# ScalarE copies the recurrence's norms out of PSUM and its kk rows into PSUM, in place of VectorE

## What is computed

```python
sa = jnp.einsum('bhij,bhj->bhi', state, -kk_t)
state = w_t[..., None] * state + sa[..., None] * (kk_t * a_t)[:, :, None, :] + k_t[..., None] * v_t[:, :, None, :]
norm = jnp.sqrt(jnp.mean(state * state, axis=-1, keepdims=True))
state = state / (norm + EPS_STATE)
o_t = jnp.sum(state * r_t[..., None], axis=-1)
```

## Time and profile before

| what | value |
|---|---|
| median of 3 runs | 2438.33 us (2436.32 to 2439.18) |
| the profiled execution's own time | 2441.28 us |
| its span in the profile | 2439.2 us |
| granted clock of TensorE, mean | 0.815 |
| VectorE busy | 2187.4 us (90% of the span) |
| ScalarE, GpSimd busy | 1585.6 us (65%), 903.2 us (37%) |

### The profile page before, as it was taken

The page is one execution under the profiler, slowest core; times in us unless marked ns, Lnnn a source line. Parts: engine busy times, 40 slices in busy tenths (PEclk is TensorE's granted clock), DMA queues, the critical chain, the costliest instruction groups (busy, mean ns, idle before and its releaser), DMA issues.

```text
span 2439.2 us, 47897 instructions
## 1 busy us (share of the span) xinstructions
PE 1925.3 (79%) x12321; PEld 1556.6 (64%) x12321; DVE 2187.4 (90%) x8800; ACT 1585.6 (65%) x5168; POOL 903.2 (37%) x1528
## 2 busy tenths in 40 slices
PE   5888888788888878888888878688887877344787
PEld 3555555455687867777777767677777767343555
DVE  6888887689619999999999999999999999999887
ACT  4878888577646665666666666666666565444776
POOL 0000000011105555555555555555555555555110
PEclk8999999699977787787877777987778777655899
DMA  5000000000000000000000000000000000000011
GB/s 183 17 17 22 17 21 23 3 1 1 1 1 1 1 1 1 1 1 1 1 1 1 1 1 1 1 1 1 1 1 1 1 1 1 1 1 1 1 35 35
DMA packets 14353, 25.02 MB, mean 10 GB/s; under 512 B 1280, under 2 KB 12032, under 8 KB 13824
## 3 DMA queue, kind: packets, MB, share of 16 engines
q1 hardware_dynamic: 14080, 21.97, 3.0%
HBM read 12.27 MB, written 4.19 MB: 7 GB/s over the span
## 4 chain that ended last, share of the span: by engine, by line
DVE 57%; issue 16%; PE 15%; ACT 6%; POOL 0%; DVEq 0%; POOLq 0%; ACTq 0%
DVE pn L1563 11%; DVE bank L1579 10%; DVE U L1620 8%; DVE xs L1551 5%; DVE bank L1568 5%; DVE kv L1612 4%; PE bank L282 3%; PE bank L267 2%; ACT prob L923 2%; PE bank L585 2%; DVE bank L1609 1%; PE bank L761 1%; DVE bank L1588 1%; DVE bank L1532 1%; PE bank L632 1%
## 5 line engine op out<-in xcount | busy, mean ns | idle before, releaser
L1748 POOL TENSOR_TENSOR wu<-U,stg 128x256 f32<-128x256 f32 x512 | 318.6, 622 | 682.2 <-DVE U L1620 682.2
L750 PE MATMUL bank<-U,ident 128*128 128x128 f32 x2048 | 464.2, 399 | 81.6 <-ACT go L1064 69.3
L750 PEld LDWEIGHTS bank<-U,ident 128*128 128x128 f32 x2048 | 426.7, 238 | 121.5 <-issue 90.6
L761 PE MATMUL bank<-stack,tm 128*128 128x64 f32 x1792 | 336.4, 374 | 145.7 <-ACT tm L994 137.2
L1213 ACT ACTIVATE xs<-U 128x128 f32<-128x128 f32 x1024 | 261.5, 302 | 275.5 <-DVE U L1620 271.6
L761 PEld LDWEIGHTS bank<-stack,tm 128*128 128x128 f32 x1792 | 325.6, 284 | 162.9 <-ACT tm L994 153.0
L1563 DVE TENSOR_REDUCE pn<-xs 128x16 f32<-128x256 f32 x1024 | 377.6, 408 | 0.6 <-issue 0.2
L1701 POOL TENSOR_TENSOR kv<-stg 128x256 f32<-128x256 f32 x513 | 318.7, 621 | 0.0
L1131 ACT ACTIVATE small<-pn 128x16 f32<-128x16 f32 x513 | 110.9, 216 | 295.0 <-DVE pn L1563 295.0
L735 PE MATMUL bank<-wcat,yT 128*128 128x224 f32 x1024 | 294.6, 447 | 2.5 <-issue 2.0
L1579 DVE TENSOR_TENSOR bank<-wu,bank 128x128 f32<-128x128 f32 x1024 | 292.0, 285 | 1.1 <-POOL wu L1748 0.8
(11 more groups left out here) (214 smaller groups left out, 3567.6 us busy)
## 6 DMA issues: line engine op xcount, KB each, us to landing
out_x<-x SPq DMA_DIRECT2D x8, 512.0 KB, 2.9
x<-in_x SPq DMA_DIRECT2D x1, 3584.0 KB, 17.7
Vs<-V SPq DMA_DIRECT2D x8, 384.0 KB, 4.6
Vs<-V SPq DMA_DIRECT2D x8, 288.0 KB, 3.3
lane<-in_lanes SPq DMA_DIRECT2D x8, 256.0 KB, 3.2
wcat<-in_wcat SPq DMA_DIRECT2D x1, 1792.0 KB, 13.2
wraw<-in_w_up SPq DMA_DIRECT2D x1, 1024.0 KB, 19.6
wraw<-in_w_down SPq DMA_DIRECT2D x1, 1024.0 KB, 11.4
```

The source lines that it names most:

```text
L750: last = pe.matmul(rsum.rearrange("p (t i) -> p t i", i=HD), ident[:, :], steps[:, :, :, j], start=(j == 0), stop=(j == HD - 1))
L761: last = pe.matmul(bank[3 + g][:, e * CH:(e + 1) * CH], tm[:, g * (PB // 2) + e, :, :].rearrange("p a c -> p (a c)"), stack[:, :], start=T ...
L1748: pool.tensor_tensor(ij(wu[:, :]), ij(U[:, half if j else 1 - half, (j - 1) % STEPS, :]), col(stg[:, half, j, TW, :]), ALU.mult).then_inc( ...
```

## The change

The `sring` ring is no longer copied. ScalarE takes the logarithm of its four rows where they lie, in PSUM, twice an iteration (`log_norms`). `stg` loses its kk part: ScalarE writes four kk rows from `R` straight to PSUM (`copy_kk`) and four rows of kk times a from `stg` to PSUM (`copy_kka`), each twice an iteration. All six stand behind the squares; each waits until VectorE has made both halves of `xs` of its step, and VectorE's first `zz` (L1568) of the same step waits for it, so that the two engines do not touch the bank at the same time. To make room, other work of ScalarE and GpSimd is moved: `retention(0)` from behind the squares of step 3 to those of step 0, `retention(1)` from behind those of step 5 to the front of those of step 1, `factors` from behind step 2's to the front of step 3's, the second part of `output_rms` to the front of step 5's, `evacuate_outputs` from the end of step 7 to behind the root of the next step 0; on GpSimd `retention_add` from step 4 to step 0.

```diff
@@ -181,10 +181,10 @@
         small = sb("small", [P, 3, HD], F32, late)
         lnr, rt, lam = (small[:, i, :] for i in range(3))
         zz = bank[0][:, 0:HD * HD]
-        kkz = bank[0][:, 256:384].rearrange("p (t q j) -> p t q j", q=2, j=HD)
-        sring = bank[0][:, 384:448].rearrange("p (t i) -> p t i", i=HD)
+        kkr = bank[0][:, 256:320].rearrange("p (t j) -> p t j", j=HD)
+        kkar = bank[0][:, 320:448].rearrange("p (g t j) -> p g t j", g=2, j=HD)
+        sring = bank[0][:, 448:512].rearrange("p (t i) -> p t i", i=HD)
         rsum = bank[7][:, 256:384]
-        hist = sb("hist", [P, 2, STEPS, HD], F32, late)
         rs = sb("rs", [P, STEPS, HD], F32, late)
         ge = sb("ge", [P, STEPS, 2 * HD], F32, late)
         gl = sb("gl", [P, STEPS, 2 * HD], F32, late)
...
@@ -1080,10 +1080,14 @@
                     act.wait_ge(O["ln"], i + 1)
                     act.activation(oss[:, 1, 0:1], oss[:, 1, 0:1], ACT.Exp, scale=0.5).then_inc(O["sd"], 1)
 
-            def stage_kk(half, row):
-
-                act.activation(stg[:, half, :, TKK, :], R[:, bass.ds(row, STEPS), QKK * HD:(QKK + 1) * HD],
-                               ACT.Copy).then_inc(G["kk"], 1)
+            def copy_kk(row):
+
+                act.activation(kkr, R[:, bass.ds(row, RENORM), QKK * HD:(QKK + 1) * HD], ACT.Copy).then_inc(S["kk"], 1)
+
+            def copy_kka(half, g):
+
+                act.activation(kkar[:, g, :, :], stg[:, half, g * RENORM:(g + 1) * RENORM, TKKA, :],
+                               ACT.Copy).then_inc(S["ka"], 1)
 
             def stage_kv(half, row):
                 act.activation(stg[:, half, :, TK:TV + 1, :].rearrange("p t q i -> p t (q i)"),
...
@@ -1108,11 +1112,14 @@
                     act.wait_ge(G["f1"], k)
                     act.activation(gl[:, :, :], ge[:, :, :], ACT.Ln, bias=1.0).then_inc(G["g2"], 1)
 
-            def log_norms(k, half, last):
-
-                act.wait_ge(S["h"], last)
-                act.wait_ge(G["f2"], k)
-                act.activation(ls[:, :, :], hist[:, half, :, :], ACT.Ln).then_inc(G["ls"], 1)
+            def log_norms(g):
+
+                act.activation(ls[:, g * RENORM:(g + 1) * RENORM, :], sring, ACT.Ln).then_inc(G["ls"], 1)
+
+            def beside_sums(t1):
+
+                for e in range(2):
+                    act.wait_ge(T[e]["x"], t1)
 
             def factors(k, half):
                 act.wait_ge(G["f2"], k + 1)
...
@@ -1186,53 +1193,70 @@
                         row_it = n % 2 * CH + m * STEPS
                         row_next = (n % 2 * CH + m * STEPS + STEPS) % (2 * CH)
                         for j in range(STEPS):
-                            root(t0 + (j + 1))
+                            t1 = t0 + (j + 1)
+                            jj, g = j % RENORM, j // RENORM
+                            root(t1)
                             if j == 0:
+                                if m >= 1:
+                                    evacuate_outputs(n, m - 1)
+                                elif n >= 1:
+                                    evacuate_outputs(n - 1, NB - 1)
                                 normalise(n, m)
+                                if m == 0 and ot is not None:
+                                    act.wait_ge(O["t1c"], (2 * ot + 2) * NB)
                                 stage_batch(n, m)
                             if j == 1:
-                                act.wait_ge(G["wc"], it + 1)
                                 gates(0, it, row_it)
                                 stage_kv(1 - half, row_next)
+                                retention(1, it + 1, row_next)
                             if j == 2:
                                 evacuate_projection(n, m, 0)
                             if j == 3:
+                                factors(it, 1 - half)
                                 evacuate_features(n, m)
                             if j == 4:
                                 row_sums(it)
                                 evacuate_projection(n, m, 1)
                             if j == 5:
                                 output_rms(n, m, 0)
+                                output_rms(n, m, 1)
                             if j == 6:
                                 stage_outputs(n, m)
                                 evacuate_pairs(n, m, 0)
                             if j == 7:
                                 evacuate_pairs(n, m, 1)
                             for e in range(2):
-                                act.wait_ge(T[e]["u"], t0 + (j + 1))
+                                act.wait_ge(T[e]["u"], t1)
                                 act.activation(xs[:, e, 1, :], rows8(U[:, half, j, :], e), ACT.Square).then_inc(T[e]["sq"], 1)
                             if j == 0:
                                 if n + 1 < NCH:
                                     act.wait_ge(C["rc"], (n + 1) * NB * 2 - 2 + 2 * m)
                                 else:
                                     act.wait_ge(C["rc"], NCH * NB * 2)
-                                stage_kk(1 - half, row_next)
-                            if j == 1:
-                                log_norms(it, 1 - half, it * 2 + 1)
-                            if j == 2:
-                                factors(it, 1 - half)
-                            if j == 3:
+                                act.wait_ge(G["wc"], it + 1)
                                 retention(0, it + 1, row_next)
                             if j == 4:
                                 gates(1, it, row_it)
-                            if j == 5:
-                                retention(1, it + 1, row_next)
-                                output_rms(n, m, 1)
-                            if j == 7:
-                                evacuate_outputs(n, m)
+                            if t1 < L and (j + 1) % RENORM == 1:
+                                beside_sums(t1 + 1)
+                                act.wait_ge(S["sg"], t1)
+                                act.wait_ge(G["f2"], it + (j + 1) // RENORM)
+                                log_norms(0 if j + 1 > RENORM else 1)
+                            if t1 < L and (j + 1) % RENORM == 2:
+                                beside_sums(t1 + 1)
+                                if t1 > RENORM:
+                                    for e in range(2):
+                                        act.wait_ge(T[e]["z"], t1 - 2)
+                                act.wait_ge(G["ka"], it + 1 + g)
+                                copy_kka(half if g == 0 else 1 - half, 1 - g)
+                            if t1 < L and (j + 1) % RENORM == 3:
+                                beside_sums(t1 + 1)
+                                copy_kk(row_it + RENORM if g == 0 else row_next)
             root(L + 1)
-            log_norms(L // STEPS, 1, L // RENORM + 1)
+            act.wait_ge(S["sg"], L + 1)
+            log_norms(1)
             factors(L // STEPS, 1)
+            evacuate_outputs(NCH - 1, NB - 1)
             act.wait_ge(O["ov"], L // STEPS + 1)
             for part in range(2):
                 i8 = slice(part * HD // 2, (part + 1) * HD // 2)
...
@@ -1546,27 +1562,27 @@
                             t1 = t0 + (j + 1)
                             if jj == 0:
                                 dve.wait_ge(S["kk"], it * 2 + (g + 1))
+                                dve.wait_ge(S["ka"], it * 2 + (g + 1))
                             for e in range(2):
                                 dve.wait_ge(T[e]["u"], t0 + j)
                                 dve.tensor_tensor(ij(xs[:, e, 0, :]), ij(rows8(U[:, half if j else 1 - half, (j - 1) % STEPS, :], e)),
-                                                  row(kkz[:, jj, 0, :], i=HD // 2), ALU.mult).then_inc(T[e]["x"], 1)
-                            if jj == 1:
-
-                                dve.wait_ge(S["sg"], t0 + j)
-                                if g == 0:
-                                    dve.tensor_copy(hist[:, 1 - half, RENORM:, :], sring).then_inc(S["h"], 1)
-                                else:
-                                    dve.tensor_copy(hist[:, half, 0:RENORM, :], sring).then_inc(S["h"], 1)
+                                                  row(kkr[:, jj, :], i=HD // 2), ALU.mult).then_inc(T[e]["x"], 1)
                             for e in range(2):
                                 dve.wait_ge(T[e]["x"], t1)
                                 dve.wait_ge(T[e]["sq"], t0 + j)
                                 dve.tensor_reduce(pn[:, e, :, :].rearrange("p a i -> p (a i)"),
                                                   xs[:, e, :, :].rearrange("p a (i j) -> p (a i) j", j=HD), AXX,
                                                   ALU.add).then_inc(T[e]["pn"], 1)
+                            if jj == 1:
+                                dve.wait_ge(G["ls"], it * 2 + (g + 1))
+                            if jj == 2:
+                                dve.wait_ge(S["ka"], it * 2 + (g + 2))
```

(20 more changed lines are left out.)

29 lines of the change are left out of this document (10 added, 19 removed).

## The result

The changed kernel takes 2445.22 us (median of 20 runs, 2437.44 to 2449.1) and the kernel before 2437.56 (20 runs, 2433.23 to 2441.24). The ratio is 1.0033, with the interval [1.0025, 1.0041]: slower by a third of a per cent. That is inside the range of the prediction, but 2 us above the 2443.2 up to which it called it the same.

The account below looks back on a forecast made before the run. Bound: a serial chain of steps, nearly all on VectorE, priced by how far instructions push off the next. Terms +12.2 - 10.5 - 2.6 + 1.3 + 0.3 = +0.7 us on the median of 2438.33 gave 2439.0 us, range 2432 to 2446.

Parts of the forecast that it names:

- the ends: Before the first step and at the end of the recurrence: +0.5 for a small operation, -0.2 for a norm copy gone.
- step 1: GpSimd's addition waits for ScalarE's exponential and delays `wu`: 3.13 us instead of 2.94, +12.2 us, bounds +9.6 and +16.0.
- steps 3 and 7: Row copies gone between reciprocal and product: 104 places at 0.06, 24 at 0.18, -10.5 us, bounds 0 and -18.7.
- step 5: Norm copy gone, but late squares hold the sums: 0.04 us won per iteration, -2.6 us, bounds 0 and -9.0.
- third wait of xs: Third semaphore at `xs` of steps 0 and 4: 0.01 us at 128 places, +1.3 us, bounds 0 and +3.8.
- Rival A: Product in steps 3 and 7 gains nothing, starting some 0.10 behind the reciprocal's end: 2445.2 us, chance 0.14.
- small delays that add up: Other delays, such as ScalarE late at step 0's squares or GpSimd slower to wake: 2443 to 2447 us, chance 0.08.
- rival D: Squares on time in step 5, so the whole 0.14 us is won there: 2432.6 us, chance 0.09.
- The steps costed at nothing: ScalarE's six new operations, hidden beside the sums before `zz`, and the moved `evacuate_outputs`, +1.6 us at most in 16 iterations.
- the prediction's own sign of error: If `zz` waits for ScalarE in steps 1 to 3 or 5 to 7, something taken as hidden is not.
- B: The addition doesn't hold `wu`, step 1 is 2.80 us and +12.2 becomes -9.0: 2417.8 us, chance 0.03.
- C: Each VectorE copy taken away in steps 3, 5 and 7 gives back all its drawn time: 2404.1 us, chance 0.02.

Follow-up runs that it names:

- few_waits: Changed kernel without the two kk row waits at the first `xs` of steps 0 and 4, except the very first: 2441.2 us, ratio 1.0008 to the kernel before.
- add_late: Changed kernel with GpSimd's `retention_add` moved from behind step 0's outer product to behind step 1's: 2424.12 us, ratio 0.9942 to the kernel before.
- wait_alone: Kernel before, all VectorE copies kept, with only both retention operations and GpSimd's `retention_add` moved as in the change: 2449.98 us, ratio 1.0050.
- u_first: Changed kernel with all three waits of `xs` in steps 0 and 4 kept, the state's written first: 2438.86 us, ratio 1.0004 to the kernel before.
- best: both_evac with the root's two waits turned round and, at the sums, the wait for the squares written before that for `xs`: 2388.61 us, ratio 0.9811.
- norms_only: Kernel before with only the norm copies removed, ScalarE taking the logarithm straight from `sring`; no retention moved: 2423.2 us, ratio 0.9939.
- root_order: Kernel before with ScalarE's root waiting for the sums of half 1 first in the code, then half 0: 2413.02 us, ratio 0.9912.
- both_evac: Changed kernel with `retention_add` behind step 1's outer product, row waits at `xs` dropped, `evacuate_outputs` back behind step 7's squares: 2415.46 us, ratio 0.9899.

## Why the prediction was where it was

The picture was right: a serial chain, a saving on VectorE and a new wait in step 1 that about cancel. The forecast of no measurable change was not right: the sum was too low by 6 to 7 us of 2440. The terms, with what the step means of the runs gave, times 64 (the ends, +0.3, weren't measured apart):

```
                          predicted   measured
step 1                      +12.2      +13.6  (few_waits against before; +14.1 with the waits)
steps 3 and 7               -10.5      -11.8  (few_waits against before)
step 5                       -2.6       -2.4  (few_waits against before; -3.0 with the waits)
third wait of xs             +1.3       +4.7  (after against few_waits, all steps)
steps 0, 2, 4, 6             none       +3.0  (few_waits against before)
```

**Step 1**, the mechanism, was right in each link, and is shown by taking it away (add_late) and by making it alone (wait_alone). In most iterations where ScalarE is on time the step is 3.12 to 3.13 us, the number predicted. The mean is higher for two reasons. In chunks 2 and 4, where the evacuation and `normalise` both stand ahead of the squares of step 0, these start 0.02 into step 1 and not 0.08 ahead of it (in seven iterations of eight), and the chain behind them shifts: 3.216 and 3.201 there. That is some 0.08 x 16 = 1.3 us, and wait_alone, with the evacuation at its old place, doesn't have it. The prediction had put this at nothing with a bound of +1.6, and had named these 16 iterations; it should have taken the bound, since it already knew that they were the first link of a chain that had become critical. The other 0.9 us come from three single places in chunks 3 and 6 (two of 3.47, one of 3.32 us), which u_first repeats to within 0.01 us.

**Steps 3 and 7** were right in mechanism and nearly in size. In the 104 places the product comes 0.284 behind the reciprocal (mean) and not 0.350, which is 0.035 after the reciprocal's end, and its second half 0.208 behind the first and not 0.191. In the 24 places with a 256-element sum between, step 7 went from 3.673 to 3.815 us down to 3.483 to 3.603, a gain of 0.19 to 0.21 with the costlier `xs` included. So Rival A is refuted, whose time, 2445.2, is by chance the measured one: it reaches it by a product that gains nothing, while the product gained and other terms were too small. Even this hit in the number is no evidence for its reason. What came is nearest to the case that stands beside A, small delays that add up (2443 to 2447, chance 0.08). Of the two that it names, only the late squares showed; the larger one, the third wait, stood in the sum itself, too small.

**Step 5** was right: the squares held the sums, and rival D, 0.14 won there, is refuted with 0.04 to 0.05.

**The third wait** is the step that failed. The prediction wrote 0.01 us for it "since rows of before don't price that". But they did give a hint: the paragraph on rival A knew that the sums start 0.10 and L1579 0.11 after what releases them, with two semaphores, and that an instruction of VectorE starts 0.04 behind another. I read these as one engine's latency against another's. Measured, the term is 4.7 / 128 = 0.037 us a place and not 0.01. few_waits and u_first show that the order of the three waits makes most of it: 0.020 at the end of steps 3 and 7 and 0.011 in the step behind (medians), 4.0 us in all. Most of the rest lies in single places that differ by more than 0.1 us. The bound of +3.8 was still too low by a microsecond.

**The steps costed at nothing**: the row copies of ScalarE beside the sums were covered (they end some 0.25 us before `zz` in the changed kernel), and so was the evacuation but for the 1.3 us in step 1. The logarithm was covered in step 1. In step 5 the prediction's own sign of error did show: `zz` waits for it in 52 of 64 iterations of the changed kernel, 0.02 us each, harmless only because the root comes later still; in best it is not harmless. Steps 0, 2, 4 and 6 are together 3.0 us longer even without the waits (few_waits against before). It isn't a little everywhere: place against place the median difference is 0.001 us or less in each of these four steps, and the 36 of 256 places that differ by more than 0.1 us, some longer and some shorter, sum to +3.3 us. Such places stay where they are from run to run while the code there is the same: in wait_alone one of these 256 moved by more than 0.1 us against the kernel before, in add_late none against the changed one. The list of waits has idle time of VectorE in the recurrence that ends for no reason it can show ("issue"), 3.2 us in 14 places before, 6.2 in 27 after and 4.8 in 21 in few_waits. What holds VectorE there no row says. This stays open.

**Rivals B and C.** B is refuted by step 1 (3.16, not 2.80), C by the pitches. For C the halves give a second proof: the norm copies, drawn at 0.21 us and 128 of them, would be worth 27 us by the drawn time, and norms_only gained 10.4. The Trainium skill, page "VectorE: DVE Perf Modes", section "The DRAIN you can't avoid", says that a following instruction waits until the pipeline is empty, and adds that one that isn't held starts earlier. These traces show a VectorE instruction start after the end of the one in front where it waits for its result (`xs` 0.04 behind the copy it reads the earlier trace rows); two halves of `U`, drawn at 0.28 us each, start 0.20 apart.

## What to carry to other kernels

Before moving work into another engine's list, ask which instruction stands behind it there: an addition of 0.46 us put in front of `wu`, waiting for a third engine, cost more than all the copies taken out of the critical engine had brought, and one place further on it was free. Price a removed instruction by the pitch of its neighbours, with and without it, not by its drawn length. And write the wait that comes last in time first in the code: here that order alone, at the root, was worth 0.9%. At the sums of step 5 it was worth nothing, though they did start earlier, because a small operation that had been hidden till then came last instead. L1595 in step 1 waits for `wu` by a wait written second; its order wasn't tried.

## What the runs showed of the hardware

How long an instruction with several waits stays behind its last releaser depends on the order in which the waits are written. If the one that comes last is written first, the instruction starts 0.03 us after the releaser's end (medians: 0.034 for the logarithm in root_order, 0.032 for the late sums behind the squares in best). If it is written second, it is 0.09 to 0.10 (0.094 for the same logarithm before, 0.102 for the same sums in both_evac). That was seen on two engines, ScalarE and VectorE.

The traces also show where the second wait goes. The wait written first stands in the instruction itself. The other one is a semaphore instruction of its own in front of it: for the root in the kernel before it is L1130, 0.017 us long, and it holds the wait for the sums of half 1; in root_order it holds the one for half 0. For the `xs` of the changed kernel it is L1567, which holds two waits and takes 0.050 us.

Whether this is seen in the time depends on what else holds the instruction. `xs` starts 0.198 us behind the second half of `U` in all steps of the kernel before, whether it has one wait or two with the state's written second. With three it is 0.218, and with the state's first of three it is 0.198 again (u_first).
